# The first two and the last four of sixteen images convolved unstacked, the ten between stacked with one transfer per 32 channels

## The reference

```python
x = x + _L0_conv_ref(_gn(x), L0_conv_W)          # 3x3 convolution, 32 groups of 4 channels
x = x + _L1_conv_ref(_gn(x), w_qkv, b_qkv, rpb, w_proj, b_proj)   # 7x7 neighbourhood attention, 16 heads of 8
```

## Time and profile before

| | |
|---|---|
| median of 3 runs | 1065.13 us (1064.41 to 1065.5) |
| the profiled execution's own time | 1068.84 us |
| its span in the trace | 1066.8 us |
| mean granted TensorE clock | 0.87 of full |
| TensorE matmuls busy | 952.5 us (89%) |
| DVE / ScalarE / POOL busy | 822.3 / 642.4 / 484.6 us |
| convolution stage | to about 242 us |
| attention stage | from there to the end |

### The profile page before, as it was taken

The page is one execution under the profiler, slowest core; times in us unless marked ns, Lnnn a source line. Parts: engine busy times, 40 slices in busy tenths (PEclk is TensorE's granted clock), DMA queues, the critical chain, the costliest instruction groups (busy, mean ns, idle before and its releaser), DMA issues.

```text
span 1066.8 us, 41868 instructions
## 1 busy us (share of the span) xinstructions
PE 952.5 (89%) x16669; PEld 630.3 (59%) x16669; DVE 822.3 (77%) x2117; ACT 642.4 (60%) x1808; POOL 484.6 (45%) x847
## 2 busy tenths in 40 slices
PE   4899997777899999999999999989999999999985
PEld 3455542235666666666676666656666666666763
DVE  4377876755879787887888787868897878788875
ACT  2111033205687868787777767666878686868653
POOL 7000002324474746464655555554647474646431
PEclk9755557678999989999899889998999898999997
DMA  9955555965555657474756465746665665737331
GB/s 233 218 161 134 136 135 148 285 185 172 165 152 167 192 142 202 118 227 103 215 144 203 117 191 143 209 118 186 163 180 155 166 186 147 205 99 226 104 87 39
DMA packets 131136, 175.00 MB, mean 164 GB/s; under 512 B 33624, under 2 KB 109944, under 8 KB 127616
## 3 DMA queue, kind: packets, MB, share of 16 engines
q1 hardware_dynamic: 125056, 157.94, 54.3%
q10 hardware_dynamic: 4608, 10.35, 3.8%
q0 software_dynamic: 1280, 4.05, 1.3%
HBM read 83.64 MB, written 67.55 MB: 142 GB/s over the span
## 4 chain that ended last, share of the span: by engine, by line
PE 64%; DVE 13%; issue 8%; ACT 7%; DMA 4%; ACTq 2%; SPq 2%; POOL 0%; DVEq 0%
PE PS L1453 14%; PE PS L1492 10%; PE PS L1476 8%; PE PS L1381 7%; PE PS L1398 6%; PE PS L1469 6%; PE PS L1435 5%; DVE area L1187 3%; DVE S L1208 3%; ACT area L845 3%; PE PS L1415 3%; ACT S L937 2%; DVE masked L1219 2%; PE PS L1502 2%; PE PS L1346 1%
## 5 line engine op out<-in xcount | busy, mean ns | idle before, releaser
L727 POOL TENSOR_TENSOR late<-masked 128x48 f32<-128x48 f32 (+1 forms) x512 | 152.6, 299 | 371.0 <-DVE masked L1219 359.7
L937 ACT ACTIVATE S<-S 128x384 f32<-128x384 f32 (+1 forms) x512 | 282.4, 554 | 25.2 <-DVE S L1208 21.8
L1208 DVE TENSOR_TENSOR S<-PS,bias 128x384 f32<-128x384 f32 (+1 forms) x512 | 282.4, 552 | 2.5 <-PE PS L1453 0.4
L1453 PE MATMUL PS<-area 97*128 97x48 bf16 (+1 forms) x4096 | 250.2, 208 | 37.9 <-DVE S L1208 32.7
L1198 DVE TENSOR_REDUCE mcol<-PS 128x6 bf16<-128x480 f32 (+2 forms) x288 | 176.1, 612 | 128.6 <-PE PS L1476 128.4
L930 ACT ACTIVATE VT<-PS 128x128 f32<-128x128 f32 x448 | 131.9, 294 | 182.6 <-PE PS L1435 179.2
L1453 PEld LDWEIGHTS PS<-area 97*128 97x128 bf16 x4096 | 179.0, 103 | 85.3 <-DVE S L1208 40.7
L1492 PE MATMUL PS<-S,VT 128*18 128x48 f32 x8192 | 197.0, 215 | 6.5 <-issue 5.9
L1492 PEld LDWEIGHTS PS<-S,VT 128*18 128x18 f32 x8192 | 117.4, 100 | 133.1 <-issue 66.2
L1476 PEld LDWEIGHTS PS<-area 128*128 128x128 bf16 x1568 | 144.9, 156 | 23.0 <-issue 8.7
L1435 PE MATMUL PS<-cst,area 128*128 128x128 f32 x448 | 141.9, 317 | 12.5 <-ACT VT L930 11.6
(11 more groups left out here) (102 smaller groups left out, 1017.9 us busy)
## 6 DMA issues: line engine op xcount, KB each, us to landing
area<-k_parts SPq DMA_DIRECT2D x32, 1008.0 KB, 7.1
area<-q_parts SPq DMA_DIRECT2D x64, 294.0 KB, 8.2
k_parts<-area SPq DMA_DIRECT2D x32, 504.0 KB, 8.1
k_parts<-area SPq DMA_DIRECT2D x32, 336.0 KB, 3.8
q_parts<-area SPq DMA_DIRECT2D x32, 294.0 KB, 7.3
area<-padded ACTq DMA_DIRECT2D x63, 112.2 KB, 3.9
out<-area SPq DMA_DIRECT2D x18, 392.0 KB, 4.1
late<-x_mid SPq DMA_DIRECT2D x17, 392.0 KB, 5.1
```

Source lines behind the costliest of these rows:

```text
L727: nc.gpsimd.tensor_tensor(sel[:, c % SEL_RING, :, :, t0:t0 + count], m[:, :, 0], m[:, :, 1], ALU.add).then_inc(s["summed"], 1)
L937: nc.scalar.activation(S[:, n % 4, 0:cols], S[:, n % 4, 0:cols], ACT.Exp).then_inc(s["probs"], 1)
L1208: nc.vector.tensor_tensor(S[:, n % 4, 0:cols], PS[:, SCORE + n % 2, 0:cols], bias[:, at:at + cols], ALU.add).then_inc(s["biased"], 1)
L1453: last = mm(PS[:, SCORE + n % 2, cols * g:cols * (g + 1)], key_rows[a][0:PEAK_ROW + 1, g, key:key + 128], query_rows[a][0:PEAK_ROW + 1, :, ...
```

## The change

1. `stacked(m)` says which images are stacked: 2 to 11. Images 0, 1, 12, 13, 14 and 15 take the nine dense matmuls from `padded[m % 2]`, and are not copied.
2. A copy is one transfer for each block of 32 channels, 4 for an image in place of 12. Its source names every partition's row three times, shifted by 0, 1 and 2. A channel's three shifts so lie in neighbouring partitions (3 x channel + shift), and `wstack` is loaded with a step of 3 partitions to match, and masked in one instruction of 96 partitions in place of three of 32.
3. `wconv` is loaded by 4 transfers in place of 9, and masked ahead of the inverse roots of the first statistics, no longer behind the padding of images 0 and 1.
4. ScalarE's 16 small loads of biases move into slots 5, 7, 9 and 11, the preparation of the projection's weights into slot 13.
5. `turn_patch` moves behind the second row of the slot's convolution.

```diff
+        FIRST_STACKED, LAST_STACKED = 2, 11
+        FIRST_LATE, FIRST_BY_SCALAR = 10, 13
...
+        BIAS_LOADS = {5: (0, 1), 7: (2, 3), 9: (4, 5), 11: (6, 7)}
...
-        def copy_image(eng, m, tiles):
-
+        def stacked(m):
+            return FIRST_STACKED <= m <= LAST_STACKED
+
+        def copy_tiles(eng, m, tiles):
+
+            if not stacked(m):
+                return
             eng.wait_ge(s["padded_ready"], m + 1)
-            if m > 2:
+            if m > FIRST_STACKED + 1:
                 eng.wait_ge(s["conv"], 2 * m - 2)
...
             for t in tiles:
-                for dc in range(3):
-                    eng.dma_start(copies(m)[t][32 * dc:32 * dc + 32, 0:SPAN], padded[m % 2][32 * t:32 * t + 32, dc:dc + SPAN]
-                                  ).then_inc(s[f"copies_in{m % 2}"], 16)
+                block_of = padded[m % 2][32 * t:32 * t + 32, 0:SPAN]
+                shifts = bass.AP(block_of.tensor, block_of.offset, [list(block_of.ap[0]), [1, 3], [1, SPAN]])
+                eng.dma_start(copies(m)[t][0:96, 0:SPAN], shifts).then_inc(s[f"copies_in{m % 2}"], 16)
...
-            for tap in range(9):
-                pool.dma_start(wconv[:, tap, :], conv_w[tap // 3, tap % 3].unsqueeze(0).broadcast_to([CH // NORM_GROUP, NORM_GROUP, CH])
-                               ).then_inc(s["wconv_in"], 16)
+            for i in range(NORM_GROUP):
+                taps = conv_w[:, :, i, :].rearrange("r t o -> (r t) o").unsqueeze(0).broadcast_to([CH // NORM_GROUP, 9, CH])
+                pool.dma_start(wconv[i:CH:NORM_GROUP, :, :], taps).then_inc(s["wconv_in"], 16)
...
             moments(0)
             spreads_of_groups(0)
+            dve.wait_ge(s["wconv_in"], 16 * NORM_GROUP)
+            nc.vector.tensor_tensor(wconv[:, :, :], wconv[:, :, :], group.unsqueeze(1).broadcast_to([128, 9, CH]), ALU.mult
+                                    ).then_inc(s["wconv_ready"], 1)
             inverse_roots(0)
...
                 if row == 0:
-                    if m:
-                        pe.wait_ge(s[f"copies_in{m % 2}"], 192 * ((m + 1) // 2))
-                        pe.wait_ge(s["wstack_ready"], 3)
+                    if stacked(m):
+                        pe.wait_ge(s[f"copies_in{m % 2}"], 64 * (m // 2))
+                        pe.wait_ge(s["wstack_ready"], 1)
                     else:
-                        pe.wait_ge(s["padded_ready"], 1)
+                        pe.wait_ge(s["padded_ready"], m + 1)
                         pe.wait_ge(s["wconv_ready"], 1)
...
-                for k in patches_at(h):
-                    turn_patch(k)
                 for at in (h, h + 0.5):
...
                     patch_scores(0, peaks[1])
+                for k in patches_at(h):
+                    turn_patch(k)
                 convolve(h, 2)
```

More of the change, by code:

```diff
@@ L605, in _ @@
             for h in range(SLOTS):
-                if h % 2 == 0 and h // 2 + 1 < IMAGES:
-                    copy_image(sp, h // 2 + 1, range(0, 2))
+                if h % 2 == 0 and h // 2 + 1 < FIRST_BY_SCALAR:
+                    copy_tiles(sp, h // 2 + 1, range(0, 2))
                 if 2 * X_RING + h < IMAGES:
@@ L694, in _ @@
                 pool.dma_start(table[i], rows.rearrange("h a b -> (a b) h"), allow_slow_non_contiguous=True).then_inc(s["table_in"], 16)
[L695 to L698, removed]
+            for dr in range(3):
+                for dc in range(3):
+                    taps = conv_w[dr, dc].unsqueeze(0).broadcast_to([32 // NORM_GROUP, NORM_GROUP, CH])
+                    pool.dma_start(wstack[dc:96:3, dr, :], taps).then_inc(s["wstack_in"], 16)
             for i in range(2):
@@ L829, in _ @@
             root(0)
[L830 to L836, removed]
             def misc(k):
@@ L976, in _ @@
                         keep_input(TURN_FROM + h, side)
-                    if h % 2 == 0 and h // 2 + 1 < IMAGES:
-                        copy_image(act, h // 2 + 1, range(2 + side, 3 + side))
+                    if h % 2 == 0 and h // 2 + 1 < FIRST_BY_SCALAR:
+                        copy_tiles(act, h // 2 + 1, range(2 + side, 3 + side))
+                if h % 2 == 0 and FIRST_BY_SCALAR <= h // 2 + 1 < IMAGES:
+                    copy_tiles(act, h // 2 + 1, range(4))
+                if h in BIAS_LOADS:
+                    for d in BIAS_LOADS[h]:
+                        load_biases(d)
+                if h == 13:
+                    prepare_weights()
                 if h == 14:
@@ L1244, in _ @@
                 pad_image(i)
-            dve.wait_ge(s["wconv_in"], 16 * 9)
-            nc.vector.tensor_tensor(wconv[:, :, :], wconv[:, :, :], group.unsqueeze(1).broadcast_to([128, 9, CH]), ALU.mult
-                                    ).then_inc(s["wconv_ready"], 1)
             split_table()
@@ L1254, in _ @@
                     dve.wait_ge(s["wstack_in"], 16 * 9)
-                    for dc in range(3):
-                        rows = slice(32 * dc, 32 * dc + 32)
-                        own = wstack[rows, :, :].rearrange("p r (t o) -> p (r t) o", o=32)
-                        nc.vector.tensor_tensor(own, own, group[rows, rows].unsqueeze(1).broadcast_to([32, 12, 32]), ALU.mult
-                                                ).then_inc(s["wstack_ready"], 1)
+                    blocks = wstack[0:96, :, :].rearrange("p r (t o) -> p (r t) o", o=32)
+                    own = cst[0:96, C_STACK:C_STACK + 32].unsqueeze(1).broadcast_to([96, 12, 32])
+                    nc.vector.tensor_tensor(blocks, blocks, own, ALU.mult).then_inc(s["wstack_ready"], 1)
                 for k in chain_at(h, 1):
```

22 lines of the change are left out of this document (15 added, 7 removed).

## The result

| | median, us | executions | lowest to highest |
|---|---|---|---|
| before | 1063.26 | 12 | 1058.66 to 1066.80 |
| after | 1068.62 | 12 | 1063.70 to 1075.53 |
| after / before | 1.0053 | | 95% interval 1.003 to 1.0076 |

The change makes the kernel slower by 0.5%, about 5.4 us. The forecast of 1068.6 us stood beside 1065.13 for the kernel before, so 3.5 us slower; the sign is right, and the size too within what can be measured. That its terms were right does not follow: one was too small, one counted a loss as a gain, and of some no run shows the worth. A ratio with an interval leaves out executions more than 1.5% above the fastest of their kernel, a median takes in all.

A forecast was written before the change was run, and what follows sets the result against it. TensorE at 1.2 GHz was taken to bound 56 to 156 us, an engine chain to 200, late copies to 242. Terms -1.5 - 1.9 - 2.0 - 1.5 - 1.4 + 11.8 = +3.5 us gave 1068.6 us, range 1060 to 1076.

The forecast's parts named there:

- part 1: Start: first convolution no longer waits for the `wconv` mask, and ScalarE's small issues go; -1.5 us.
- its own signs: Wrong if last stretch much below 50 us, slots from 56 to 156 us under 7.8, or slot 24 over 13 earlier.
- Part 6: Last four images, unstacked: 53.8 us of TensorE work with no waits, against 42.0 us before; +11.8 us.
- rival D: Last eight half images run at 1.2 GHz and cost 47.6 us more, 1116 us; chance 0.03.
- Part 2: Image 1, slots 2 and 3: 14.6 us unstacked instead of 16.5 with the wait for copies; -1.9 us.
- Part 3: Slot 4 onwards: TensorE arrives with its clock up, worth between nothing and 3.9 us; middle taken, -2.0 us.
- rival A: Slots 4 to 16: clock stays up while bias tables are picked, DVE becomes the bound, 1051.2 us; chance 0.10.
- Parts 4 and 5: Slots 16 to 18 and 20 to 23: root waits go, also TensorE's for rounded patches; -1.5 and -1.4 us.
- rival C: Merged transfers land late for images 10 and 11, or the start doesn't move; 1076 us; chance 0.14.

The follow-up runs named there:

- cut versions: All sixteen convolutions, attention of four images only; medians: before 452.01, changed 460.68, last images stacked 449.17, patches early 453.68, both undone 445.48, image 1 stacked besides 452.44 us.
- four executions named above: Four of six timed executions of the cut changed kernel with last images stacked, patches turned early and image 1 stacked: between 452.06 and 453.87 us.
- cut pair: Profiled executions of the kernel before and the changed one, both with attention of four images only: 456.65 and 458.03 us.
- 1st pair: First full-length profiled executions, unedited: kernel before 1068.84 us, changed kernel 1063.70 us.
- 2nd pair: Both full-length kernels profiled once more, unedited, on another chip: before 1076.86 us, changed 1065.56 us.
- eight edited versions: Changed kernel with last images stacked, image 1 stacked, patches early, or both undone (1056.13, 1076.64, 1065.36, 1053.85 us), and four edited versions with attention of four images only.
- last chip: Chip of the third group of runs, with the unedited kernel before beside the edited versions: median 1062.78 us over 23 executions.

## Why the prediction was right, and where it was not

The medians of the cut versions make a ladder from the kernel before to the changed one: 452.0 us; with the merged transfers, the new start and the moved bias loads 452.4; with image 1 unstacked 445.5; with the patches turned late 449.2; with the last four images unstacked 460.7. The steps are +0.4, -7.0, +3.7 and +11.5, in sum +8.7 us; at full length the sum is +5.4. Only the last step is firm. The first three cross from one chip to another or hang on the four executions named above, and their intervals take in 0.

Three pairs of traces stand beside it, of the kernel before and the changed one: the first, the second, and the cut pair. Each number is by how much a stretch got shorter or longer.

| part | forecast | 1st pair | 2nd pair | cut pair | by times |
|---|---|---|---|---|---|
| 1, to slot 1's add | -1.5 | -4.5 | -3.8 | -3.2 | |
| 2, to slot 3's | -1.9 | -2.7 | -2.0 | +4.0 | parts 2 and 3 together -7.0, -8.0 |
| 3, to slot 16's | -2.0 | -6.7 | -5.4 | -6.5 | |
| 4 and 5, to slot 24's start | -2.9 | -3.3 | -3.9 | -1.6 | with part 1: +0.4 + 3.7 |
| 6, to the last add | +11.8 | +12.0 | +8.0 | +8.4 | +11.5, +11.5 |
| sum | +3.5 | -5.2 | -7.1 | +1.1 | +5.4 (+8.7 cut) |

The changed kernel is steady in these traces, with its last add at 236.7, 238.9 and 238.6 us. The kernel before is not: 241.9, 246.0 and 237.6.

By its own signs the forecast failed in two places although the total came out: slot 24 started 17.2 us earlier than 199.94, where 13 was the limit, and a slot behind 56 us took 5.8 us (56.80 to 62.58 between adds), where 7.8 was. The second sign was badly set, since the kernel before has a slot of 6.1 us there itself (129.09 to 135.21).

*Part 6 was right about the new stretch*, to 0.3 us: from slot 24 to the last add it took 54.0, 54.0 and 54.1 us against the 53.8 worked out from the earlier trace rows; the clock stayed at 1.00 and TensorE waited for nothing, so rival D fell. The gain from removing the waits for copies was counted inside the 42.0 us of before, and that made the sign. The 42.0 itself was a short case: it was 46.0 and 45.7 in the two other traces of the kernel before. The times, +11.5 twice, compare with the changed kernel whose last images are stacked again, in which the stretch took 41.7 to 46.0 us in four traces.

*Part 2 was right* about the slots after: 35.43 to 50.06, 14.6 us, as forecast. The slots before were read 0.9 us short: their last turned pieces start at 56.41 and end at 57.35, so it was 17.5 and the part gives 2.8. Beside the cut kernel before, which kept its clock there, it costs 4.0.

*Part 3 was mis-sized.* "I take the middle, -2.0 us" between nothing and one slot of full clock was wrong, since the clock lasted two slots in most traces and three in the first, to about 70 us: between slot 3's add and slot 16's the traces have 92.6, 94.0 and 94.0 us instead of 99.4, 99.4 and 100.5. The step should have been priced by rival A's own bound, DVE: TensorE at the full clock is faster than DVE there, so it starts to wait, and the clock goes some slots later. Rival A was thus true for 10 to 20 us and false for the rest. The Trainium skill (TensorE: Matmul & The Clock Gate, the part on the clock gate) puts the fall down to idle time, and the trace agrees for this fall: 11.58 of 16 us busy between 56 and 72 us, and half the clock from then on. The same part gives an engine that is busy the upper level, and there the trace differs: from 72 to 156 us TensorE was busy 83.65 of 84 us at a mean of 0.54.

*Parts 4 and 5 counted a loss as a gain.* For the patches the forecast said that TensorE "no longer stands 7.2 us in five places", and took 1.4 us of it as gain. The waits did go, down to 1.9 us once. But TensorE's wait came back as 3.96 us for a copy, in a worse place, and DVE's as 10.0 us for the patches. Turning them late cost 7.0 us (3 to 9.5) between two cut kernels on one chip, and 2.3 to 3.7 us in the other three comparisons, whose intervals take in 0; the stretch to slot 24 got shorter in all three pairs even so, by 1.6 to 3.9 us. The bounds "between 0 and the full 7.2" did not allow for a loss at all, although the move puts TensorE's turning behind two of three rows of the convolution, for which DVE waits in the same slot. That is rival C's place (images 10 and 11), but not its mechanism.

*What the merged transfers and the start give is open.* The first convolution starts 3 to 4 us earlier in every trace after the change, and DVE's waits for the roots are gone, yet the medians of the cut versions put the two together at nothing (+0.4, interval -9 to +4).

*Why traces and times differ is open too.* The three profiled executions of the kernel before, and of its cut, lie 5.6, 13.5 and 4.6 us above the medians of their timed ones; those of the changed kernel and of its cut lie 4.9 and 2.6 below, and those of the eight edited versions between 4.6 below and 3.8 above. A cost that recording lays upon many small transfers would explain it, since the kernel before issues twelve an image and the others four; but no run has small transfers and is otherwise the changed kernel, so this was not tested. A second explanation is on record: the two full-length traces of the kernel before have mean clocks of 0.870 and 0.874, and timed executions of it at 0.865 to 0.871 took 1073.3 to 1075.3 us on the last chip. So the traces may show the kernel before in its slower executions, with the long standstill, and the times take in those without it. That covers the first trace; the second, 1076.86 us, is still 4 us above every timed execution on its chip.

The total was right, then, largely by luck: a term of +11.8 that the times confirm, and around it an image 1 that gave more than forecast in two of three pairs of traces and late patches that cost some us instead of giving 1.4, which offset each other.

## What to carry to other kernels

Price a change of form where it runs: unstacking image 1 at the start removed a standstill and bought some twenty us of full clock in most traces, while the same code in the last four images gave 12.1 us of idle time for 24.1 us more of TensorE (54.0 busy instead of 29.9). A removed wait is a gain only once the next thing to be late is known, so ask, of each instruction that is moved behind others, who waits for it on the other engine. And hold the profiled execution against the timed ones before its trace is used to explain half a per cent: here two pairs of traces had the sign wrong, and the third showed an execution of the kernel before that the first two did not.

## What the runs showed of the hardware

The spread of one kernel goes with its granted clock. On the last chip, the kernel before took 1073.3 to 1075.3 us in the four executions whose mean clock was 0.865 to 0.871, and 1054.0 to 1061.7 in the eight at 0.889 to 0.895. A kernel that runs the same instructions can thus vary by 2%.

Where a standstill lies counts beside how long it is: 3.52 us ahead of slot 21, against 1.91 us in it and 3.92 ahead of slot 22, left slots 22 and 23 mostly at 2.4 or at 1.2 GHz, and the stretch to slot 24 at 8.48 or 13.56 us.

The length of a standstill alone does not tell whether the clock falls. Ahead of the stacked slot 2 it stayed at 1.00 after 1.99 us (cut kernel before) and fell to 0.50 after 1.87 and 2.13 us (the two versions with image 1 stacked). Ahead of slot 6, where TensorE waited for DVE, it fell behind 0.96 or 0.97 us in eight traces and stayed up behind the same 0.96 us in the ninth. Once down it did not come back in 28.00 of 28 busy us (72 to 100 us, changed kernel).
